# Row attention inside a fused kernel: four heads' matmuls interleaved on TensorE, another order of the row's work, and negated scores

## The reference, cut to what matters

```python
x = x + L0(_gn(x), ...)      # layer 0, below
x = x + L1(_gn(x), ...)      # layer 1: convolution, four scans, gate; untouched

def L0(x, mask, ln_w, ln_b, w_tri, w_q, w_k, w_v, w_g, b_g, w_o, b_o):
    xn = (x - mu) * rsqrt(var + EPS) * ln_w + ln_b
    tri_bias = einsum('bijd,dh->bhij', xn, w_tri)[:, None]
    mask_bias = 1e9 * (mask[:, :, None, None, :] - 1.0)
    q = (xn @ w_q).reshape(B, I, J, H, C) * (1.0 / sqrt(C))     # H = 4, C = 32
    k, v = (xn @ w_k).reshape(...), (xn @ w_v).reshape(...)
    scores = einsum('bimhc,binhc->bihmn', q, k) + tri_bias + mask_bias
    attn = softmax(scores, axis=-1)
    o = einsum('bihmn,binhc->bimhc', attn, v)
    g = sigmoid((xn @ w_g + b_g).reshape(B, I, J, H, C))
    return (g * o).reshape(B, I, J, H * C) @ w_o + b_o
```

## Time and profile before

| | us |
|---|---|
| median of 3 runs | 29268.55 (29249.78 to 29271.03) |
| the profiled execution, its own time | 29284.73 |
| its span, first to last instruction | 29282.9 |
| attention: first to last writing of `xo1` | 747.2 to 4576.5, 256 rows |

### The profile page before, as it was taken

How to read it: one execution, slowest core, us unless ns; L and a number is a source line. 1 busy time by engine, 2 the same in 40 slices (tenths; PEclk the granted TensorE clock), 3 DMA queues, 4 the chain that set the end, 5 groups by cost and what they waited for, 6 DMA issues and landing times.

```text
span 29282.9 us, 495306 instructions
## 1 busy us (share of the span) xinstructions
PE 23746.5 (81%) x145198; PEld 17788.1 (61%) x145198; DVE 25685.0 (88%) x24511; ACT 23805.4 (81%) x48778; POOL 23349.3 (80%) x10372
## 2 busy tenths in 40 slices
PE   5999995888888888887888888888878888888887
PEld 1656563666666666666666666666666666666666
DVE  7555555999999999999999999999999999999999
ACT  2444444998889899888888888898888888998888
POOL 4000003999999999999999999999999999999999
PEclk6999997999999999999999999999999999999999
DMA  4000003333333333333333333333333333333333
GB/s 143 26 27 26 26 27 139 108 106 106 107 106 108 106 107 106 106 107 107 106 106 106 105 108 106 107 106 106 107 107 106 107 106 107 106 106 108 106 108 97
DMA packets 2189273, 2869.65 MB, mean 98 GB/s; under 512 B 695002, under 2 KB 964858, under 8 KB 2177786
## 3 DMA queue, kind: packets, MB, share of 16 engines
q1 hardware_dynamic: 2181978, 2803.33, 31.2%
q10 hardware_dynamic: 4608, 33.82, 0.3%
HBM read 2667.01 MB, written 169.74 MB: 97 GB/s over the span
## 4 chain that ended last, share of the span: by engine, by line
ACT 27%; PE 25%; issue 16%; DVE 11%; POOL 3%; ACTq 1%; DVEq 1%; DMA 0%; SPq 0%; POOLq 0%
DVE hst L1535 10%; PE yps L1245 8%; ACT dbT L1425 6%; ACT dAs L1403 6%; ACT dA L1403 6%; PE dbx L1230 5%; PE misc L1145 5%; PE misc L1164 2%; POOL hc L1612 2%; POOL dbu L1598 1%; DVE hc L1543 1%; ACT vab L1358 1%; PE misc L1181 1%; PE cps L1221 1%; ACT vab L1344 1%
## 5 line engine op out<-in xcount | busy, mean ns | idle before, releaser
L1598 POOL TENSOR_TENSOR dbu<-dtu,bb 128x1024 f32<-128x1024 f32 x4096 | 9686.7, 2371 | 1217.2 <-DVE hst L1535 1215.0
L1535 DVE TENSOR_TENSOR_SCAN hst<-dA,dbu 128x1024 f32<-128x1024 f32 x4096 | 9347.6, 2282 | 773.1 <-ACT dA L1403 750.2
L1612 POOL TENSOR_TENSOR hc<-hst,cc 128x1024 f32<-128x1024 f32 x4096 | 9728.0, 2375 | 5.1 <-DVE hst L1535 4.0
L1245 PE MATMUL yps<-ident,hc 128*128 128x128 f32 x65536 | 8945.1, 283 | 333.0 <-POOL hc L1612 329.7
L1245 PEld LDWEIGHTS yps<-ident,hc 128*128 128x128 f32 x65536 | 7986.0, 147 | 1823.7 <-issue 1273.3
L1535 DVE TENSOR_TENSOR_SCAN hst<-dAs,dbx 128x1024 f32<-128x1024 f32 x3584 | 8117.8, 2265 | 58.8 <-issue 57.1
L1230 PE MATMUL dbx<-ident,dbT 128*128 128x128 f32 x28672 | 4153.1, 292 | 3343.6 <-DVE hst L1535 2977.8
L1230 PEld LDWEIGHTS dbx<-ident,dbT 128*128 128x128 f32 x28672 | 3391.2, 148 | 4764.1 <-DVE hst L1535 3652.8
L1425 ACT ACTIVATE dbT<-dtuT,bT 128x256 f32<-128x256 f32 x14336 | 6126.1, 495 | 18.2
L1403 ACT ACTIVATE dA<-dtv,aneg 128x508 f32<-128x508 f32 x8192 | 5291.6, 678 | 405.6 <-DVE hst L1535 402.1
L1403 ACT ACTIVATE dAs<-dtv,aneg 128x508 f32<-128x508 f32 x7168 | 4743.5, 711 | 520.1 <-DVE hst L1535 518.1
(11 more groups left out here) (188 smaller groups left out, 28222.6 us busy)
## 6 DMA issues: line engine op xcount, KB each, us to landing
bb<-l_bscr SPq DMA_DIRECT2D x1024, 1024.0 KB, 5.7
cc<-l_bscr SPq DMA_DIRECT2D x1024, 1024.0 KB, 5.5
bx<-l_bscr SPq DMA_DIRECT2D x1024, 256.0 KB, 6.1
xg<-xgp SPq DMA_DIRECT2D x512, 85.0 KB, 2.5
xgp<-xb ACTq DMA_DIRECT2D x32, 1032.0 KB, 9.4
xt<-in_x_dram SPq DMA_DIRECT2D x128, 256.0 KB, 2.8
l_xnT<-xo SPq DMA_DIRECT2D x128, 256.0 KB, 2.0
xn<-l_xnT SPq DMA_DIRECT2D x256, 128.0 KB, 2.1
```

Of the source, the lines that this page charges most:

```text
L1245: mm = pe.matmul(yps[:, p, f * P:(f + 1) * P], hc[:, u % HB, f * 512 + p * P:f * 512 + (p + 1) * P], ident[:], is_transpose=True, start=fi ...
L1535: nc.vector.tensor_tensor_scan(hst[:, v % 4, way], decays.rearrange("p f c -> p (f c)")[:, way], inputs.rearrange("p f c -> p (f c)")[:, way],
L1598: nc.gpsimd.tensor_tensor(to, dtu[:, step % 2], row.unsqueeze(1).to_broadcast([P, 2, 512]), ALU.mult).then_inc(s_inp, 1)
L1612: nc.gpsimd.tensor_tensor(hc[:, v % HB].rearrange("p (f c) -> p f c", f=2), hst[:, v % 4].rearrange("p (f c) -> p f c", f=2), row.unsqueez ...
```

## The change

TensorE gets another order: scores of all four heads are issued with the head as the inner loop, so that neighbouring calls use different 32-row strips of the array, then the sums of all heads, again with the head inside, so that neighbours use different 32-column strips. `output(r-2)` moves up behind `project(r)`, and `turn_factors` behind the sums. The waits are per row, not per head: `scores` waits for all four `pT` copies, and `sums` has the same copies behind it. The scores are computed with a negated sign (q scaled by -1/sqrt(32), bias and mask negated before), so that VectorE reduces with a minimum straight into `nmx`, `minus` goes, and the exp takes scale -1. The gate is 0.5 * (1 + tanh(x/2)): Tanh on ScalarE, a reciprocal of the eight sums per partition, `(ge + 1) * rse`, and the 0.5 in the copy to `fT`. Three `pT` copies are on VectorE (0, 2, 3), now ahead of `vv` and `ge`; one on ScalarE. ScalarE writes `xo1` ahead of the row's exps.

```diff
-                    def sums(r, h, d):
+                    def sums(r, h):
+                        wait(pe, s_gs, r)
+                        pe.wait_ge(s_ve, r * 2 + 1)
+                        pe.wait_ge(s_tv, r * 3 + 3)
+                        pe.wait_ge(s_ta, r + 1)
                         for k in range(NT):
-                            mm = pe.matmul(ps_o[HD * d:HD * d + HD, 0:N], vv[:, h, k, HD * d:HD * d + HD], pT[:, d, k],
-                                           start=(k == 0), stop=(k == NT - 1))
-                        if d == NH - 1:
-                            mm.then_inc(s_o, 1)
-                    def scores(r, h, d):
...
-                        wait(pe, s_ta if d % 2 else s_tv, r * 2 + (d // 2 - 1))
+                            for d in range(NH):
+                                mm = pe.matmul(ps_o[HD * d:HD * d + HD, 0:N], vv[:, h, k, HD * d:HD * d + HD], pT[:, d, k],
+                                               start=(k == 0), stop=(k == NT - 1))
+                        mm.then_inc(s_o, 1)
+                    def scores(r, h):
+                        pe.wait_ge(s_mk[h], NH * turns(r, h, 1))
+                        pe.wait_ge(s_qe, r + 1)
+                        wait(pe, s_tv, r * 3)
+                        wait(pe, s_ta, r)
                         for a in range(NT):
-                            dst = banks[:, 2 + d, a * N:(a + 1) * N]
-                            rows_d = slice(HD * d, HD * d + HD)
-                            pe.matmul(dst, qk[rows_d, h, 0, a * P:(a + 1) * P], qk[rows_d, h, 1, :], start=True, stop=False)
-                            mm = pe.matmul(dst, ones3[HD * d:HD * d + 3], mrow[HD * d:HD * d + 3, h], start=False, stop=True)
-                        mm.then_inc(s_sc, 1)
+                            for d in range(NH):
+                                rows_d = slice(HD * d, HD * d + HD)
+                                pe.matmul(banks[:, 2 + d, a * N:(a + 1) * N], qk[rows_d, h, 0, a * P:(a + 1) * P], qk[rows_d, h, 1, :],
+                                          start=True, stop=False)
+                            for d in range(NH):
+                                mm = pe.matmul(banks[:, 2 + d, a * N:(a + 1) * N], ones3[HD * d:HD * d + 3], mrow[HD * d:HD * d + 3, h],
+                                               start=False, stop=True)
+                                if a == NT - 1:
+                                    mm.then_inc(s_sc, 1)
...
                     def turn(r, h, stages):
                         if "new" in stages:
                             project(r, h)
+                        if "end" in stages:
+                            output(r - 2, h)
                         if "mid" in stages:
                             turned(r - 1, 1 - h)
-                        for d in range(NH):
-                            if "mid" in stages:
-                                sums(r - 1, 1 - h, d)
-                            if "new" in stages:
-                                scores(r, h, d)
-                            if "mid" in stages and d == 1:
-                                turn_factors(r - 1)
-                        if "end" in stages:
-                            output(r - 2, h)
+                        if "new" in stages:
+                            scores(r, h)
+                        if "mid" in stages:
+                            sums(r - 1, 1 - h)
+                            turn_factors(r - 1)
...
-                            nc.scalar.activation(ge[:, h], ge[:, h], ACT.Exp, scale=-1.0).then_inc(s_ge, 1)
+                            nc.scalar.activation(ge[:, h], ge[:, h], ACT.Tanh, scale=0.5).then_inc(s_ge, 1)
...
                         dve.wait_ge(s_ex, r * NH + NH)
+                        nc.vector.reciprocal(rse[:], se[:, h]).then_inc(s_dn, 1)
...
-                        dve.wait_ge(s_dn, r * 2 + 1)
-                        nc.vector.reciprocal(den[:], den[:]).then_inc(s_dn, 1)
...
                     def turn(r, h, stages):
+                        if "mid" in stages:
+                            for d in (0, 2, 3):
+                                dve.wait_ge(s_tf, r * NH + (d + 1 - NH))
+                                wait(dve, s_o, r - 1)
+                                nc.vector.tensor_copy(pT[:, d].rearrange("p k n -> p (k n)"), banks[:, 2 + d]).then_inc(s_tv, 1)
...
-                                                                          1.0, -3.0e38, ALU.add, ALU.max, mx[:, h, d, a:a + 1])
+                                                                          1.0, 3.0e38, ALU.add, ALU.min, nmx[:, h, d, a:a + 1])
                                 last.then_inc(s_sm, 1)
-                                if d:
-                                    minus(r, h, d - 1)
-                            minus(r, h, NH - 1)
```

More of the change, by code:

```diff
@@ L326, in layer0 @@
             se = sc("se", [P, 2, NT, NH])
+            rse = sc("rse", [P, NT, NH])
             fT = sc("fT", [P, N])
@@ L458, in turn_factors @@
                     def turn_factors(r):
                         pe.wait_ge(s_dn, r * 2 + 2)
-                        wait(pe, s_xe, r - 1)
+                        wait(pe, s_xe, r)
                         for a in range(NT):
@@ L501, in turn @@
                             wait(act, s_sc, r * NH - NH)
[L502 removed]
+                            nc.scalar.mul(qk[:, h, 0], ps_qk[:, 0:N], float(-1.0 / HD ** 0.5))
                             nc.scalar.copy(qk[:, h, 1], ps_qk[:, N:2 * N]).then_inc(s_qe, 1)
[L504 to L505 removed]
                         if "mid" in stages:
[L507 to L521 removed]
+                            act.wait_ge(s_tf, r * NH + (2 - NH))
+                            wait(act, s_o, r - 1)
+                            nc.scalar.copy(pT[:, 1].rearrange("p k n -> p (k n)"), banks[:, 3]).then_inc(s_ta, 1)
                         if "end" in stages:
@@ L526, in turn @@
                             nc.scalar.activation(xo1[:, h], ps_x[:, N:2 * N], ACT.Identity, bias=bo[:]).then_inc(s_xe, 1)
+                        if "new" in stages:
+                            act.wait_ge(s_ve, r * 2 + 2)
+                            nc.scalar.activation(ge[:, h], ge[:, h], ACT.Tanh, scale=0.5).then_inc(s_ge, 1)
+                        for d in range(NH):
+                            if "mid" in stages and d == 1:
+                                act.wait_ge(s_gt, r)
+                                wait(act, s_gs, r - 1)
+                                nc.scalar.mul(fT[:], ps_x[:, 0:N], 0.5).then_inc(s_fc, 1)
+                            if "new" in stages:
+                                act.wait_ge(s_sm, r * NH + (d + 1))
+                                for a in range(NT):
+                                    last = nc.scalar.activation(ss[:, h, d, a], ss[:, h, d, a], ACT.Exp, scale=-1.0, bias=nmx[:, h, d, a:a + 1],
+                                                                accum_out=se[:, h, a, d:d + 1])
+                                last.then_inc(s_ex, 1)
                     all_rows(act, turn)
@@ L561, in turn @@
                         if "mid" in stages:
-                            for d in (0, 2):
-                                dve.wait_ge(s_tf, r * NH + (d + 1 - NH))
-                                wait(dve, s_o, r - 1)
-                                nc.vector.tensor_copy(pT[:, d].rearrange("p k n -> p (k n)"), banks[:, 2 + d]).then_inc(s_tv, 1)
                             factors(r - 1, 1 - h)
```

37 lines of the change are left out of this document (4 added, 33 removed).

## The result

The changed kernel takes 27609.35 us (median of 4 runs, 27602.55 to 27622.95), against 29269.79 of before: a ratio of 0.9434, 95% interval 0.9417 to 0.945.

The account below looks back on a forecast made before the run. TensorE was taken to bound the attention row: passes 12.35, shape changes 0.45 and copy wait 1.17 make 13.97 us; less 3.42 for overlap 10.55, with clock 10.75 against 15.02, 1093 us saved. Forecast 28180 us, range 27700 to 29100.

Parts of the forecast that it names:

- What bounds the kernel: Attention row before the change: TensorE sets it, 14.80 us at full clock, of which 12.35 are passes.
- The walk of the softmax chain: From first score pass through reduction and exps: reduction to first exp 0.73 us, ScalarE's exps done at 8.6 us.
- Fewer changes of shape: TensorE's row: three changes of shape in place of some ten cost 0.45 us instead of 1.5, 1.05 saved.
- The wait for the copies: TensorE before the scores: waiting for all four pT copies takes 1.17 us, replacing 0.95, so 0.2 lost.
- Heads side by side: Scores, masks and sums: partial overlap of heads in different strips, limited by order of starts, saves 3.42 us a row.
- A: Scores and sums: all four heads run at once, scores bound by weight loads; 9.25 us a row, 27800 us; chance 0.14.
- B: Only one kind overlaps: scores alone give 28580 us, sums alone 28680 us; chance 0.13.
- What is late next: Softmax chain behind the scores: ScalarE's exps end 0.4 us early, so TensorE keeps the row by a thin margin.
- The clock: TensorE's granted clock in the attention, 0.97 before: its cost stays as now, 0.2 us a row.
- Rival D: Attention: longer transposes and wait, 2.9 us, make the clock fall to 0.50; at three quarters of rows 29720 us; chance 0.09.
- The sum: Attention row: 10.55 us plus 0.2 for the clock is 10.75 against 15.02, 1093 us less over 256 rows.
- The arithmetic: VectorE and ScalarE work, 6.6 and 6.7 us a row, fits under 10.5 and costs nothing; cover gone below about 9.

Follow-up runs that it names:

- e9: Kernel before the change, only each head's negation moved right behind its own reductions: 29047 us (eight runs), ratio 0.9933.
- e2: Changed kernel with the head as the outer loop in the sums only: 27637 us, ratio 0.9438.
- e10: Changed kernel with the head outermost in the sums and every sum matmul issued twice: 28401 us, ratio 0.9698.
- e6: Changed kernel with output(r-2) moved behind the transposes, just ahead of the scores: 27472 us, ratio 0.9384.
- e1: Changed kernel with the head as the outer loop in the scores and their masks only: 28547 us, ratio 0.9749.
- e3: Changed kernel with the head as the outer loop in both scores and sums: 28551 us, ratio 0.975.
- e5: Kernel before the change with the new arithmetic alone, all orders as before: 29089 us, ratio 0.9935.
- e4: Changed kernel with the old arithmetic (maximum and negation, Exp gate, large reciprocal), new order kept: 28082 us, ratio 0.959.

## Why the prediction was wrong

**What bounds the kernel.** That a row was TensorE's was right in the main, but not complete. The wait of 0.95 us before the sums was put down to the copies. It was the tail of a longer chain, which began with the negation standing one head late (e9, 0.8 us a row). The walk of the softmax chain missed it because it paired the reduction at 4.33, head 1's, with the exp at 5.22, head 0's. The 0.73 us that it took from this pair lies near the 0.81 of the changed kernel (2008.00 to 2008.81) by luck: two reductions and a handover lie between in either case.

**Fewer changes of shape.** Right. Three are left: the scores are 1.29 where their passes are 1.08, the sums 1.01 where they are 0.86, the factors' block 0.27 where it is 0.22. Together 0.41, for a stated 0.45.

**The wait for the copies.** Right: 2006.61 less 2003.75 + 1.75 is 1.11, for 1.17.

**Heads side by side.** This is the step that failed. The text took the order of starts for a rule, and so let only one pass of a head run beside the next head's: five steps for eight passes, nine for sixteen, 3.42 us saved. Measured, the scores' passes fall from 4.33 to 1.08 and the sums' from 3.45 to 0.86, 5.84 us. The order of starts in the records of before was a consequence of the program, where neighbours always shared a strip or changed the shape. It said nothing on strips that differ. e2 shows passes starting ahead of others that precede them in the program; e10 gives the limit, three passes waiting in a strip.

**The rivals A and B.** B, only one kind overlapping, is out: both blocks run four heads at once. A bounded the scores at eight loads of 0.11 in a row, 1.0 a half. Wrong as well: four loads of four strips take the time of one. A's 27800 was for that reason, and for the clock that it kept, still too slow, though its mechanism, strips that do not wait for each other, is what happened. Its pace agrees in direction with the Trainium skill's "TensorE: Matmul & The Clock Gate", Part 3, but here the factor is 4.0 for four row strips and four column strips alike, counted in passes, in place of 3.07 for four row strips and 2.38 for three column strips. The same part of the Trainium skill says that matmuls keep program order in start and end; the starts in e2 and e10 do not agree with that for passes in different strips.

**What is late next.** ScalarE's chain was not the next bound, as stated. But the loop over VectorE's reductions, the gating and the output was not walked. TensorE waits for it 0.35 us in the row shown (2011.26 less 2010.05 + 0.86) and 0.44 in the mean of 1200 to 2800 us; e6 took it out together with the wait for the copies and gained 0.56 us a row.

**The clock.** Its share was to stay at 0.2 us a row. It went: the granted clock is 1.00. Rival D named the stretch of transposes and wait, 2.9 us in a shorter row. That stretch exists in the changed kernel, 2003.75 to 2006.61, and no fall follows. The falls returned with the staggered scores (0.78 in e1 and e3), with the same transposes and the same wait. So the transposes and the wait alone do not make a fall; in e1 and e3 the falls come with scores that have the array to one or two row strips. It is not staggering as such, since e10's staggered sums kept 1.00, and it is not the passes alone: in the old order, with the same blocks on TensorE, the clock was 0.97, 0.98 (e5) and 0.94 (e9). What else decides it is open. The Trainium skill's rule in "TensorE: Matmul & The Clock Gate", Part 4, that transposes count for less, would have made the falls more frequent here; no run shows that, and the changed kernel, with the longer stretch in every row, has 1.00.

**The sum.** From the forecast's 10.75: 2.42 less for the overlap (5.84 for 3.42), 0.20 for the clock, 0.10 for shape changes and copies, and 0.44 more for the wait for the gating, gives 8.47 against 8.59 measured.

**The arithmetic** was priced at nothing. By the four corners it is worth 190 us alone (e5), and 472 behind the new order (28082 less 27609); the order alone 1202 (29284 less 28082), and 1480 behind the new arithmetic. These times hold what the later stages did too: from first to last scan they took 24397 us in e5 and 24387 in e4, against 24347 before and 24349 in the changed kernel. In the attention alone the rows are 15.02 before, 14.09 in e5 ((4334.9 - 742.5) / 255), 10.25 in e4 ((3340.8 - 728.0) / 255) and 8.59, so that the arithmetic is worth some 238 us alone and 425 behind the new order. The forecast had warned that VectorE's cover would be gone "below about 9 us a row", and the row went below it; no run tests that figure.

## What to carry to other kernels

When matmuls use only a strip of the array, the order in the program decides whether strips overlap. Interleave so that no strip gets more than four passes before the others have theirs; that is the count at which e2 still overlapped fully and e1, with six, did not. An order of starts read from a trace in which nothing could overlap is no rule for one in which it can; where a page and such a row disagree, keep both ends and weigh them alike. And before taking an operation to be as cheap as its own length, ask what is queued ahead of it: a negation of 0.17 us, one head late, cost 0.8 us a row.

## What the runs showed of the hardware

- Different 32-row or 32-column strips run fp32 passes of 256 columns together, four for the time of one, starts 7 ns apart in the records of the changed kernel. The weight loads of four row strips overlap too, four within 0.20 us.
- A strip behaves as if it held three waiting passes beside the running one; the next pass for it blocks all later ones (0.893 us between strips in e10, 0.54 in e1).
- TensorE's granted clock in the attention was 0.97 before, 1.00 with four strips together, 0.78 with staggered scores (e1, e3), and 1.00 with staggered sums (e10).
- A stage whose code is untouched changed by up to 149 us (24317 to 24466) with what ran ahead of it, in the same way in every run of a kernel, together with its granted clock.
